# Weighing each image of a pair in its own 64-row tile: a deformable convolution's loop, re-cut between three engines

## The reference

```python
offset = conv2d(x, off_w, off_b)                       # (dy, dx) for each of 9 taps
mask = sigmoid(conv2d(x, mask_w, mask_b))
samp = deform_sample(x, offset, mask)                  # bilinear, (B, C, 9, H, W), zero outside
out = einsum('bckhw,ock->bohw', samp, weight.reshape(O, C, 9)) + bias
```

## Time and profile before

| | us |
|---|---|
| median of three runs | 611.6 |
| the profiled execution, whole | 613.81 |
| its span, first to last instruction | 612.0 |
| PE busy | 461.5 (75%) |
| DVE busy | 358.7 (59%) |
| ACT busy | 289.4 (47%) |
| POOL busy | 93.4 (15%) |
| mean granted TensorE clock | 0.879 of full |

### The profile page before, as it was taken

One profiled execution on the slowest core, in us unless ns is written; L12 is line 12 of the kernel. 1 busy time (PEld: TensorE's weight loads), 2 busy tenths in 40 slices (PEclk: granted clock), 3 DMA queues, 4 the chain that ended last, 5 costly groups with the idle time before them and its releaser, 6 DMA issues. The chain is left out here.

```text
span 612.0 us, 9607 instructions
## 1 busy us (share of the span) xinstructions
PE 461.5 (75%) x2946; PEld 222.7 (36%) x2946; DVE 358.7 (59%) x676; ACT 289.4 (47%) x471; POOL 93.4 (15%) x79
## 2 busy tenths in 40 slices
PE   2318633999997373585899999839387999999994
PEld 1106522544553132132455555315132333333331
DVE  5358765123645967763899999240544555656564
ACT  0569941222234152052566666604646467485441
POOL 6700012000000035000000000010025136062000
PEclk9758975999999767586999999959587999999999
DMA  5300004200000015533200000037380370732202
GB/s 141 95 1 0 0 0 107 64 1 0 0 0 0 0 32 164 158 94 106 72 3 1 1 1 1 2 99 186 86 173 5 84 149 6 179 47 58 58 1 69
DMA packets 22555, 34.33 MB, mean 56 GB/s; under 512 B 5360, under 2 KB 17792, under 8 KB 21760
## 3 DMA queue, kind: packets, MB, share of 16 engines
q1 hardware_dynamic: 22528, 33.99, 22.6%
HBM read 16.97 MB, written 4.64 MB: 35 GB/s over the span
## 5 line engine op out<-in xcount | busy, mean ns | idle before, releaser
L1228 DVE TENSOR_TENSOR L_s<-L_row_ps,L_cols 128x1024 f32<-128x1024 f32 x72 | 88.1, 1225 | 74.5 <-ACT L_cols L1279 74.5
L943 ACT ACTIVATE L_e<-L_ring 128x512 f32<-128x512 f32 x128 | 71.7, 596 | 67.3 <-PE L_ring L988 66.6
L866 DVE TENSOR_REDUCE L_mx<-L_ring 128x2 f32<-128x512 f32 x128 | 82.7, 684 | 29.7 <-PE L_ring L977 28.3
L1352 PE MATMUL L_acc<-L_s,L_t_sb 128*64 128x256 f32 x576 | 79.7, 399 | 5.1 <-DVE L_s L1228 5.1
L1279 ACT ACTIVATE L_cols<-L_col_ps 128x512 f32<-128x512 f32 x72 | 42.7, 594 | 56.9 <-PE L_col_ps L1342 56.9
L977 PE MATMUL L_ring<-stacks_k_st,stacks_q_st 128*128 (+1 forms) x256 | 54.9, 301 | 12.5 <-DMA stacks_k_st<-L_k_parts 8.5
L988 PE MATMUL L_ring<-stacks_q_st,stacks_k_st 128*128 (+1 forms) x128 | 49.9, 395 | 15.8 <-DMA stacks_q_st<-L_m_parts 15.6
L1329 PE MATMUL L_col_ps<-all_w_all,L_xn 128*128 128x384 f32 x96 | 46.8, 581 | 15.2 <-ACT L_t_sb L1283 10.9
L1352 PEld LDWEIGHTS L_acc<-L_s,L_t_sb 128*64 128x64 f32 x576 | 35.5, 138 | 53.3 <-DVE L_s L1228 31.1
L1339 PE MATMUL L_row_ps<-L_hats,L_sel 48*128 48x512 bf16 x144 | 43.6, 384 | 2.2 <-DMA L_hats<-L_parts 2.2
L632 PE MATMUL L_xs_ps<-L_stack,L_w_tap 128*128 (+1 forms) x96 | 44.1, 600 | 0.0
(11 more groups left out here) (246 smaller groups left out, 671.6 us busy)
## 6 DMA issues: line engine op xcount, KB each, us to landing
L_hats<-L_parts SPq DMA_DIRECT2D x32, 216.0 KB, 4.9
L_hat<-L_offsets SPq DMA_DIRECT2D x24, 192.0 KB, 3.7
stacks_q_st<-L_q_parts SPq DMA_DIRECT2D x48, 64.0 KB
stacks_k_st<-L_k_parts SPq DMA_DIRECT2D x24, 128.0 KB
L_stack<-L_xpad SPq DMA_DIRECT2D x16, 162.0 KB, 3.1
L_stack<-L_xpad SPq DMA_DIRECT2D x16, 153.0 KB, 3.1
L_mask<-L_offsets SPq DMA_DIRECT2D x12, 192.0 KB, 4.0
L_q_parts<-L_parts SPq DMA_DIRECT2D x8, 192.0 KB, 3.0
```

What stands on the lines that cost most here:

```text
L866: dve.tensor_reduce(mx[:, b, :, head], ring[:, k % 2].rearrange("p (q s) -> p q s", q=2), AX.X, ALU.max).then_inc(max_read, 1)
L943: act.activation(e[:, k], ring[:, 2 + k % 2], ACT.Exp, scale=HD2 ** -0.5).then_inc(e_ready, 1)
L1228: dve.tensor_tensor(s[:, q], row_ps[:, q], cols[:, q:q + 1].broadcast_to([P, 2, 2 * N]), ALU.mult).then_inc(s_ready, 1)
L1352: mm = pe.matmul(acc[C * e:C * e + C, b, 0:N], t_sb[:, b, h, (KK * e + t) * C:(KK * e + t + 1) * C], s[:, q, h, e * N:(e + 1) * N], start= ...
```

## The change

Layer 3's weighing is cut by image. `w_all` holds one copy of the weights for each half of the rows instead of a block-diagonal matrix, `TW` falls from 384 to 192, and each step is two products of 64 rows and 192 columns: image 0 into the free second half of an `acc` bank, image 1 into `col_ps`. ScalarE copies image 1's result only; VectorE copies image 0's (`take_first_image`), ahead of its product of the same tap. The weighing taps move from (0, 2, 3, 5, 6, 7) to (1, 2, 3, 5, 6, 7). The hats of the two pairs have a semaphore each, and SP no longer waits for them to land; at the start the hats of both first pairs are sent in a row, ahead of the loads of the next chunk. `send_stack` issues half of its DMAs on SP and half on ScalarE's queue, in layers 1 and 3.

```diff
-WEIGHED = (0, 2, 3, 5, 6, 7)
+WEIGHED = (1, 2, 3, 5, 6, 7)
-def send_stack(sp, xpad_ready, stack_in, xpad, stack):
+def send_stack(eng, e, xpad_ready, stack_in, xpad, stack):
     for g in range(NQ):
-        sp.wait_ge(xpad_ready, 2 * g + 2)
+        eng.wait_ge(xpad_ready, 2 * g + 2)
...
-        for e in range(2):
-            sp.dma_start(dst[0:C, :, e, :], src[C * e:C * e + C]).then_inc(stack_in[g], 16)
-            sp.dma_start(dst[C:P, :, e, 0:(HP - 1) * WP], src[C * e:C * e + C, :, WP:HP * WP]).then_inc(stack_in[g], 16)
+        eng.dma_start(dst[0:C, :, e, :], src[C * e:C * e + C]).then_inc(stack_in[g], 16)
+        eng.dma_start(dst[C:P, :, e, 0:(HP - 1) * WP], src[C * e:C * e + C, :, WP:HP * WP]).then_inc(stack_in[g], 16)
             @block.scalar   # layer 1 (edge_ready 3) and layer 3 (edge_ready 2)
                 gn.scalar(act)
+                act.wait_ge(edge_ready, 2)
+                send_stack(act, 1, xpad_ready, stack_in, xpad, stack)
...
-    TW = 2 * KK * C // 3
+    TW = KK * C // 3
...
-                def send_hats(n, b):
+                def send_hats(b):
                     for k in range(2):
                         for e in range(2):
                             first = C * k + 2 * b + e
-                            sp.dma_start(hats[...], parts[first:C * k + C:CH]).then_inc(hats_in, 16)
-                    sp.wait_ge(hats_in, 64 * n + 64)
-                    sp.sem_inc(passed, 1)
+                            sp.dma_start(hats[...], parts[first:C * k + C:CH]).then_inc(hats_in[b], 16)
...
-                send_hats(0, 0)
+                send_hats(0)
+                send_hats(1)
                 sp.wait_ge(off_stored, 128)
                 sp.wait_ge(mask_stored, 128)
                 for j in range(3):
                     load_positions(1, j)
                     load_masks(1, j)
-                send_hats(1, 1)
...
+                def take_first_image(b, w, k):     # VectorE
+                    dve.wait_ge(first_ready, w + 1)
+                    dve.tensor_copy(t_sb[:, b, k // 3, ds(k % 3 * TW, TW)], acc[:, b, N:N + TW]).then_inc(first_read, 1)
                 for hat_step, j in hat_split(dve):
                     hat_step(0, j)
+                for k in range(6):
+                    take_first_image(0, k, k)
                 dve.sem_inc(s_ready, 2)
...
                     for t in range(1, KK):
+                        if t - 1 in WEIGHED and more:
+                            k = WEIGHED.index(t - 1)
+                            take_first_image(1 - b, 6 * n + 6 + k, k)
                         sample(n, b, t, 7 + 15 * n + col_step(t - 1, more))
...
-                            act.wait_ge(hats_in, 128 * c)
+                        for b in range(2):
+                            act.wait_ge(hats_in[b], 64 * c)
...
-                def weigh(b, c, k, r):
+                def weigh(b, w, c, k, r):
+                    if from_turn(w, 1):
+                        pe.wait_ge(first_read, w)
                     if from_turn(c, 2):
                         pe.wait_ge(col_read, c - 1)
-                    pe.matmul(col_ps[:, r, 0:TW], xn[:, b, k // 3 * P:(k // 3 + 1) * P], w_all[:, k % 3 * TW:(k % 3 + 1) * TW],
-                              start=True, stop=True).then_inc(col_ready, 1)
+                    for e, out in ((0, acc[:, b, N:N + TW]), (1, col_ps[:, r, 0:TW])):
+                        rows = slice(C * e, C * e + C)
+                        mm = pe.matmul(out, xn[rows, b, k // 3 * P:(k // 3 + 1) * P], w_all[rows, k % 3 * TW:(k % 3 + 1) * TW],
+                                       start=True, stop=True)
+                        mm.then_inc((first_ready, col_ready)[e], 1)
...
                         if t in WEIGHED and more:
-                            if t == 0:
+                            k = WEIGHED.index(t)
+                            if k == 0:
                                 pe.wait_ge(xn_ready, n + 2)
+                                pe.wait_ge(added, n + 2)
```

More of the change, by code:

```diff
@@ L186, in __init__ @@
             dict(w_q=[P, P], w_k=[P, P], w_v=[P, P], w_o=[P, 2, C], b_v=[P, P], l2_vec=[P, 3]),
-            dict(w_off=[P, 6, 32], w_all=[P, 2 * W3 * W3 * C], sel=[P, 3, P], grid=[P, N], w_grid=[P, 32], l3_vec=[P, 3])]
+            dict(w_off=[P, 6, 32], w_all=[P, W3 * W3 * C], sel=[P, 3, P], grid=[P, N], w_grid=[P, 32], l3_vec=[P, 3])]
         self.loaded = m.sems("loaded0 loaded1 loaded2 loaded3")
@@ L484, in _ @@
                 sp.wait_ge(edge_ready, 3)
-                send_stack(sp, xpad_ready, stack_in, xpad, stack)
+                send_stack(sp, 0, xpad_ready, stack_in, xpad, stack)
             @block.gpsimd
@@ L1087, in layer3 @@
         hat_in, mask_in = m.sems("hat_in0 hat_in1 hat_in2"), m.sems("mask_in0 mask_in1 mask_in2")
-        (hats_in, xn_ready, row_ready, col_ready, col_read, s_ready, s_used, added, passed) = m.sems(
-            "hats_in xn_ready row_ready col_ready col_read s_ready s_used added passed")
+        hats_in = m.sems("hats_in0 hats_in1")
+        (xn_ready, row_ready, col_ready, col_read, s_ready, s_used, added, first_ready, first_read) = m.sems(
+            "xn_ready row_ready col_ready col_read s_ready s_used added first_ready first_read")
         def hat_split(eng):
@@ L1151, in send_hats @@
                             first = C * k + 2 * b + e
-                            sp.dma_start(hats[C * k:C * k + 3 * H, b, e, :], parts[first:C * k + C:CH]).then_inc(hats_in, 16)
-                    sp.wait_ge(hats_in, 64 * n + 64)
-                    sp.sem_inc(passed, 1)
+                            sp.dma_start(hats[C * k:C * k + 3 * H, b, e, :], parts[first:C * k + C:CH]).then_inc(hats_in[b], 16)
                 def next_chunk(i, more):
@@ L1349, in samples @@
                         pe.wait_ge(col_read, 15 * n + 6)
+                        pe.wait_ge(first_read, 6 * n + 6)
                     for h in range(2):
@@ L1357, in _, with pair @@
                 for k in range(6):
-                    weigh(0, k, k, k % 2)
+                    weigh(0, k, k, k, k % 2)
                 pe.wait_ge(off_ready, 2 * NQ)
                 pe.wait_ge(sel_ready, 1)
-                pe.wait_ge(hats_in, 64)
+                pe.wait_ge(hats_in[0], 64)
                 spread(0, 0, 0, 6, 0)
-                def pair(n, b, more, _):
+                def pair(n, b, more, chunk):
                     for t in range(KK):
@@ L1393, in pairs @@
             pair(2 * i + b, b, 2, i + 1)
-    pair(NP - 2, 0, 1, None)
-    pair(NP - 1, 1, 0, None)
+    pair(NP - 2, 0, 1, NP // 2)
+    pair(NP - 1, 1, 0, NP // 2)
 def program(nc, ins, out, layers=4):
@@ L1480, in lay_out @@
     t["w_off"] = w_off.reshape(P, 6, 32)
-    t["w_all"] = two_blocks(a["L3_conv_weight"].transpose(1, 2, 3, 0).reshape(C, -1))
+    t["w_all"] = np.tile(a["L3_conv_weight"].transpose(1, 2, 3, 0).reshape(C, -1), (2, 1))
     bias = np.concatenate([a["L3_conv_off_b"][0::2], a["L3_conv_off_b"][1::2], a["L3_conv_mask_b"]])
```

11 lines of the change are left out of this document (6 added, 5 removed).

## The result

| us | before | changed |
|---|---|---|
| median of the comparison | 612.5 (4 runs) | 598.5 (4 runs, 597.52 to 599.3) |
| span of the profiled execution | 612.0 | 597.0 |
| PE busy | 461.5 | 439.6 (74%) |
| DVE busy | 358.7 | 379.7 (64%) |
| mean granted clock of TensorE | 0.879 | 0.872 |

A forecast was written before the change was run, and what follows sets the result against it. TensorE's work bounded layer 3's loop, with the copy-product-samples-spread cycle as floor. Stack -1.2, start +0.3, pair 0 -5.7, pairs 1 to 5 -7.6, pair 6 -1.3: -15.5, from 611.6 to 596.1, stated as 596.0 us; range 590.5 to 603.

The forecast's parts named there:

- w, the weighing: Layer 3's loop: the weighing of a tap as two row-half products takes 0.50 us, against 0.84 before.
- The lower bound: The weighing in layer 3's loop with no overhead at all: 0.32 us, giving about 591 us in total.
- Tiles side by side: Layer 3's weighing: two products on different row halves run at once, 0.50 us together; the forecast's chance 0.72.
- The rival of program order: Layer 3's weighing: records start and end in program order, three turns, 0.78 us; about 605 us total; chance 0.11.
- that of tiles in turn: Layer 3's weighing: tiles run one after the other, 1.04 us, a pair 20.7; about 615 us total; chance 0.05.
- The cycle's floor: Layer 3's loop: copy, product, samples and spread repeat every 3.66 us for two taps; applied to taps 8 and 0.
- ScalarE's excess: Taps 1 to 4 of a chunk's first pair: hat steps exceed TensorE's work by 0.9 us; pair 18.2, not 17.7.
- Pair 0: First pair of layer 3's loop: -6.2 us from earlier hats and shorter weighing, +0.5 for later full clock, -5.7.
- The stack: Stack DMAs issued on two queues: -0.7 us in layer 3 and -0.5 in layer 1, -1.2 together.
- The start: Start of layer 3: pair 0's weighings and VectorE's copies alternate every 1.4 us, costing +0.3 us (0 to +2).
- The hats: Hat sends in layer 3: the second follows the first at once; of 3.0 us of later ScalarE waits 0.6 stays.
- The clock in the loop: Rival: TensorE's loop busy share falls from 97% to about 90%, bringing half clock; a quarter gives 627 us; chance 0.04.

The follow-up runs named there:

- Experiment 4: Changed kernel with both images' weighing products on rows 0 to 63 of the array, so no different row halves: 618.8 us, ratio 1.0092.
- experiment 5: Changed kernel with VectorE's norm moved from tap 4 to tap 1 in a chunk's first pair: 596.3 us, ratio 0.9722.
- experiment 10: experiment 5's kernel with ScalarE's hat steps spread out, Abs and Relu at taps 1, 3 and 5: 593.9 us, ratio 0.9694.
- experiment 6: Changed kernel with the norm at tap 4 written as scalar_tensor_tensor with a broadcast shift instead of tensor_scalar: 598.2 us (one run).
- experiment 8: Changed kernel with added, unread fp32 products on TensorE during pair 0's first weighings: 598.6 us, ratio 0.9784.
- Experiment 2: Kernel before with the weighing's change alone, hats and stack as before, run a second time for another profile: 610.57 us (one run).

## Why the prediction was near, step by step

The span was forecast to fall by 15.5 us and fell by 15.0, and that is partly luck, for terms cancel. Second pairs and pair 6 were put too dear by 3.6 us and the waits for hats by 0.6; the first pairs of a chunk, pair 0, the stack with the start, and the end were put too cheap by 2.1, 1.6, 0.8 and 0.2.

- **w, the weighing: too large.** It was put at 0.50, as 0.32 of columns and an overhead of 0.18; it measured 0.33, so there is no overhead. The lower bound was the truth. That made the six weighed taps 1.87 and not 2.04, and a second pair 16.82 and not 17.7: 0.9 us in each of pairs 1, 3 and 5, and 1.0 in pair 6. Experiment 4 speaks of where the 0.20 around the old weighing's columns sat: four records of half the length in 64-row tiles, all on one row half, stream the same 0.64 us of columns and take 0.66, while the product on 128 rows took 0.84. So it seems to have belonged to the step from the spread's tiles to a product on all rows.
- By the Trainium skill, TensorEngine Tiling (Array Packing), Key Properties, a change of tiling mode drains TensorE. By that rule w was 0.43; 0.33 and 0.66 agree with a drain of some 0.18 us that is gone. No run here changes the mode and nothing else, so this cause is argued and not shown.
- **Tiles side by side: right.** Rows of the third spread product and image 1's first are 0.01 us apart, and experiment 4 doubles the time by taking the second row half away. The rival of program order (0.78) and that of tiles in turn (1.04) are both out.
- **The cycle's floor: right for taps 8 and 0, missed at tap 4.** Read from the last pair as 1.83 us a tap, it was put under taps 8 and 0, 3.66 together; they took 3.65 to 3.76. Tap 4 stands alone between weighed taps and was put at 1.55, TensorE's work, with 0.2 a pair for late products. It took 1.80: with w at 0.33 its neighbours hide less of the cycle. In front of its product ScalarE's copy ended (475.43 + 0.60 = 476.03) no sooner than VectorE's (475.64 + 0.36 = 476.00), so the new copy on VectorE is not alone the cause.
- **A chunk's first pair: too small.** ScalarE's excess was forecast as 18.2 us; with the norm out of the way the pair takes 18.07 (experiment 5), so that term was right in size, and spreading out the hat steps took 0.4 off it (experiment 10). What the forecast lacked is VectorE's norm. It stands at tap 4, it cost 0.40 in the kernel before, and the prediction never asked what GpSimd does then. Before, GpSimd's product had 0.2 us left at that moment (499.96 + 1.81 = 501.77) and its subtraction came only at 503.41, since `take_first` was late: the norm at 501.54 ran in between. With the hats on time the subtraction follows at once, and the norm takes 2.0 us, 1.2 of which reach the pair's end. The wait for hats hid a collision.
- The Trainium skill, SBUF — State Buffer, Who interferes with whom, says that VectorE and GpSimd share one pair of SBUF ports, that `tensor_scalar` can need it in its 2-port mode, that an instruction with two SBUF inputs contends with a GpSimd instruction that reads SBUF, and that in the 2-port mode whoever issues first blocks the other fully. The 2.0 and 2.12 us beside 0.40 and 0.48 agree, as does the product L1235, which reads PSUM and takes 1.22 us whether GpSimd runs or not. Read against the hat steps' new times, the page would have pointed to this step.
- **Pair 0: 4.1 us, not 5.7.** It ran 24.27 us from spread to addition; 28.35 - 5.7 = 22.65 were forecast, 0.5 of them for a late full clock. The norm at 459.21 is 1.3 of the difference (22.93 without it, experiment 5), and 0.3 is left. The samples of both of the first taps took 1.97 us, where before only the first took 1.88. What half clock in the second tap costs can be read from experiment 6, whose norm was held as well but whose second samples had full clock:

```profile
452.69 1.08 PE L1374 MATMUL L_acc<-L_s,L_t_sb 128*64 128x256 f32 x8
```

  Its pair 0 ran 469.53 - 445.86 = 23.67 us, 0.6 less. So the 0.5 was about right. Keeping TensorE busy beforehand (experiment 8) did not keep the first samples at full clock, since TensorE idles in the first taps.
- **The stack: nothing, not -1.2.** The bound "bandwidth may hold it to nothing" was the case: the landing, not the issue, set the convolution's start, and it grew from 3.1 to 5.6 us.
- **The start: as forecast.** Weighings and copies alternate every 1.45 us (438.38, 439.83, 441.29, 442.74, 444.20; forecast 1.4), and the first spread starts at 445.42; the last copy starts 0.2 before it.
- **The hats: right.** 0.6 us of waits was left in the sum, and none was measured. But a wait for hats was reckoned at its length alone. Experiment 2 shows that without the new order the short weighing loses half clock on top, so the change's two halves are worth far more together (14 us) than apart (2.6 and 3.6 by the ratios).
- **The clock in the loop: right for the change, wrong as a rival's ground.** The rival argued from the mean busy share and was given 0.04. The changed kernel has full clock from 456 to 580 us; the weighing alone has not. In the loops of these traces half clock followed the longer waits for hats (experiment 2), while a loop that is busy 36.3 of 40 us without such a wait kept its full clock.

What stays open: 17.67 against 16.82 us in first pairs after experiment 10, where the columns' copy still comes late behind Abs and Relu; and why TensorE, busy throughout, was granted half clock for 29 us in experiment 4.

## What to carry to other kernels

When a stall is removed, list what each engine did during it, and above all which instruction of VectorE will now fall beside one of GpSimd: the stall may have kept them apart. Read the floor of a loop (here the cycle of copy, product, samples and spread) from a stretch that doesn't carry the work being cut, and check it for every part of the loop, a lone tap between two heavy ones too. Check a link of the chain of waits against the start and end times: two engines that end together can look like one waiting for the other. Two 64-row products side by side took 0.33 us here where one 128-row product with zeros in it took 0.84; both stood behind a spread in row tiles.

## What the runs showed of the hardware

- Two fp32 products of 192 columns on different row halves take 0.33 us together, on the same half 0.66.
- A matrix product later in the program starts first if its rows are free: image 1's at 482.34, image 0's at 482.55.
- VectorE's SBUF-to-SBUF instruction of 0.40 us took 2.0 when GpSimd's work closed up before and behind it, to the end of GpSimd's second instruction (495.32 + 1.99 = 497.31, against 495.52 + 1.64 = 497.16). Where only the last 0.2 us of one GpSimd instruction lay over it, it took 0.40 (the kernel before) or 0.51 in its other form (experiment 6).
- After 2.4 us of idle time in 3, TensorE ran 4 us at half clock while busy 97% (experiment 2). In experiment 4 it was busy throughout 29 us and had half clock in all of them.
- With two queues issuing the stack's DMAs at once, each lands later: 5.6 us against 3.1.
